# Delta attention: block products two at a time on 64x64 corners, all five instruction queues in a new order, and an opening block with four operand buffers

## The reference, cut to what matters

```
q, k, v = silu(short_conv(x @ Wq)), silu(short_conv(x @ Wk)), silu(short_conv(x @ Wv))
beta = 2 * sigmoid(x @ Wb);  g = -exp(A_log) * softplus(x @ Wa + dt_bias)
q = q * rsqrt(sum(q*q) + 1e-6) / sqrt(128);  k = k * rsqrt(sum(k*k) + 1e-6)
for each token t:
    S = S * exp(g_t)
    for i in range(3):
        S = S + beta_i * outer(k_i, v_i - k_i @ S)
    o_t = q_t @ S
o = o * rsqrt(mean(o*o) + 1e-5) * rms_weight * silu(x @ Wg);  y = o @ Wo
```

## Time and profile before

| | us |
|---|---|
| median of 3 runs | 3219.11 (3215.27 to 3219.3) |
| the profiled execution, its own time | 3221.68 |
| its span | 3219.9 |
| PE busy | 3008.8 (93%) |
| DVE busy | 2537.5 (79%) |
| ACT busy | 2250.6 (70%) |
| POOL busy | 1972.9 (61%) |
| the opening block ends | 78.9 |
| the loop's last output tile | 2478 |

### The profile page before, as it was taken

One profiled execution on the slowest core, in us unless ns is written; L12 is line 12 of the kernel. 1 busy time (PEld: TensorE's weight loads), 2 busy tenths in 40 slices (PEclk: granted clock), 3 DMA queues, 4 the chain that ended last, 5 costly groups with the idle time before them and its releaser, 6 DMA issues. The chain is left out here.

```text
span 3219.9 us, 83441 instructions
## 1 busy us (share of the span) xinstructions
PE 3008.8 (93%) x27212; PEld 2368.3 (74%) x27212; DVE 2537.5 (79%) x5859; ACT 2250.6 (70%) x6953; POOL 1972.9 (61%) x3125
## 2 busy tenths in 40 slices
PE   5569999999999999999999999999987999767999
PEld 3458888888888888888888888888876444455444
DVE  5669999999999999999999999999754454594554
ACT  4768888888888888888888888888643343412443
POOL 1588888888888888888888888888831000100000
PEclk8779999999999999999999999999998899967999
DMA  4457777676777667676767677777532333002322
GB/s 102 122 143 172 180 190 178 172 180 169 179 178 188 179 175 179 174 175 176 187 176 182 173 176 179 175 178 184 151 93 74 148 123 124 10 3 76 145 116 112
DMA packets 588204, 482.87 MB, mean 150 GB/s; under 512 B 464784, under 2 KB 504368, under 8 KB 581632
## 3 DMA queue, kind: packets, MB, share of 16 engines
q1 hardware_dynamic: 583552, 475.44, 55.3%
q10 hardware_dynamic: 4224, 2.10, 0.2%
HBM read 285.53 MB, written 191.86 MB: 148 GB/s over the span
## 5 line engine op out<-in xcount | busy, mean ns | idle before, releaser
L919 DVE SCALAR_TENSOR_TENSOR conv_k<-PP,tk,conv_k 128x256 f32<-128x256 f32 x1536 | 722.6, 479 | 61.0 <-ACT conv_k L754 33.3
L692 POOL TENSOR_TENSOR X<-X,tmp 96x31 f32<-96x31 f32 (+15 forms) x992 | 534.5, 539 | 77.8
L919 DVE SCALAR_TENSOR_TENSOR conv_v<-PP,tv,conv_v 128x256 f32<-128x256 f32 x1152 | 539.3, 477 | 45.0 <-ACT conv_v L754 35.3
L689 POOL TENSOR_TENSOR tmp<-At,X 96x31 f32<-96x31 f32 (+15 forms) x992 | 486.6, 491 | 63.6 <-DMA At<-n_d 5.4
L1088 PE MATMUL PP<-xn,wk 128*128 128x268 f32 x1024 | 342.7, 419 | 35.3 <-DVE conv_k L919 26.5
L675 POOL TENSOR_TENSOR rk<-ss,half 96x8 f32<-96x8 f32 x128 | 209.1, 1633 | 175.4 <-DVE ss L887 175.4
L657 POOL TENSOR_TENSOR Sg<-S,gend 128x512 f32<-128x512 f32 x256 | 266.1, 1040 | 63.3 <-DVE S L878 63.3
L726 ACT ACTIVATE recA<-TG,es 96x128 f32<-96x128 f32 x1024 | 284.8, 368 | 6.0 <-DVE es L912 6.0
L754 ACT ACTIVATE conv_k<-PP,tk 128x256 f32<-128x256 f32 x512 | 245.2, 480 | 56.2 <-PE PP L1088 49.0
L718 ACT ACTIVATE recA<-TG 128x128 f32<-128x128 f32 x1024 | 265.5, 272 | 24.5 <-PE TG L1139 24.5
L1052 PE MATMUL RB<-rhs,Yf 96*96 96x128 f32 x2048 | 269.1, 274 | 14.5 <-DVE rhs L867 14.3
(11 more groups left out here) (289 smaller groups left out, 6776.1 us busy)
## 6 DMA issues: line engine op xcount, KB each, us to landing
kqg_d<-kqgA SPq DMA_DIRECT2D x128, 512.0 KB, 6.2
kqgB<-kqg_d SPq DMA_DIRECT2D x128, 512.0 KB, 4.3
rec_d<-recA SPq DMA_DIRECT2D x128, 480.0 KB, 3.4
recB<-rec_d SPq DMA_DIRECT2D x128, 480.0 KB, 5.6
f1gates<-f1gates_d SPq DMA_DIRECT2D x24, 1024.0 KB, 6.7
f2gates<-f2gates_d SPq DMA_DIRECT2D x24, 1024.0 KB, 6.8
gdec<-gdec_d SPq DMA_DIRECT2D x128, 128.0 KB, 5.6
apk_d<-apkA SPq DMA_DIRECT2D x128, 128.0 KB, 3.3
```

Of the source, the lines that this page charges most:

```text
L689: nc.gpsimd.tensor_tensor(t, At[q % 2][:, j, j + 1:].unsqueeze(2).broadcast_to(sh), X[q % 2][:, j, 0:cols].unsqueeze(1).broadcast_to(sh), ...
L692: nc.gpsimd.tensor_tensor(x, x, t, ALU.subtract).then_inc(sub_ev, 1)
L919: return nc.vector.scalar_tensor_tensor(acc, src[:, :, j:j + SPAN], w[:, j:j + 1], acc, ALU.mult, ALU.add)
```

## The change

In the opening block: `gm` has four buffers instead of two; the fourth piece of each head's table is stored from ACT's queue instead of SP's; the order of squares, copies, turns, centring and norms of the four blocks changes. In the loop: `apkB` and `Dd` hold half of the units on partitions 64 to 127, `zm` does its products in turn on partitions 0 to 63 and 64 to 127 (inputs and outputs), its load is six DMAs instead of three, and `zev` copies in four instructions instead of two. `ss_` adds a tensor of 1e-6 (`g.tiny`) instead of the constant. All five queues have a new order in the frame; `o_(r, 1)`, `mo_(r, 1)`, `vtr(c, 0)`, `vr(c, 0)` and two spots of `subst` pass into the next frame.

```diff
-        gm = sb("gm", [128, 2, NC, TC])
+        DEEP = 4
+        gm = sb("gm", [128, DEEP, NC, TC])
...
+
+        def keep_table(eng, h, b):
+            eng.dma_start(g.edec_d[h, :, :, b, :], ex[TC * b:TC * (b + 1), h, :].rearrange("t (s x) -> t s x", x=SPAN)).then_inc(g.edec_out[h], 16)
...
         @block.sync
         def _(sp):
...
             for h in range(NH):
...
-                for b in range(B):
-                    sp.dma_start(g.edec_d[h, :, :, b, :], ex[TC * b:TC * (b + 1), h, :].rearrange("t (s x) -> t s x", x=SPAN)).then_inc(g.edec_out[h], 16)
+                for b in range(B - 1):
+                    keep_table(sp, h, b)
...
+            raw(2)
...
-            raw(2)
+            raw(3)
...
-            raw(3)
...
+            gates(2)
...
-            gates(2)
...
-                    last = nc.tensor.matmul(GE[h % 2][:, a, :], after_bd[:, :], gm[:, h % 2, 16 * a:16 * (a + 1), :], start=True, stop=True)
+                    last = nc.tensor.matmul(GE[h % 2][:, a, :], after_bd[:, :], gm[:, h % DEEP, 16 * a:16 * (a + 1), :], start=True, stop=True)
...
         @block.scalar
...
             for q in range(B):
+                square(q)
...
-                square(q)
-                if q:
-                    keep_xn(q - 1)
+                if q >= 2:
+                    keep_xn(q - 2)
+            keep_xn(B - 2)
...
             for h in range(NH):
...
+                if h:
+                    act.wait_ge(mask_ev, h)
+                    keep_table(nc.scalar, h - 1, B - 1)
+            act.wait_ge(mask_ev, NH)
+            keep_table(nc.scalar, NH - 1, B - 1)
...
         @block.gpsimd
         def _(pool):
...
+            nc.gpsimd.memset(g.tiny[:, :], 1e-6)
...
             for q in range(B):
...
             for q in range(1, B):
...
+                centre(q)
...
-                centre(q)
-                norm(q - 1)
+                if q >= 2:
+                    norm(q - 2)
+            norm(B - 2)
...
             def sums(h):
...
-                need(dve, ge_mm, h - 2)
-                nc.vector.tensor_tensor(gm[:, h % 2, :, :], gt[:, h, :].unsqueeze(2).broadcast_to([128, NC, TC]), upto, ALU.mult).then_inc(gm_ev, 1)
+                need(dve, ge_mm, h - DEEP)
+                nc.vector.tensor_tensor(gm[:, h % DEEP, :, :], gt[:, h, :].unsqueeze(2).broadcast_to([128, NC, TC]), upto, ALU.mult).then_inc(gm_ev, 1)
...
-            sums(0)
-            sums(1)
+            for h in range(DEEP - 1):
+                sums(h)
             for h in range(NH):
...
-                if h + 2 < NH:
-                    sums(h + 2)
+                if h + DEEP - 1 < NH:
+                    sums(h + DEEP - 1)
...
 
         kqgB = two("kqgB", [128, U, 128])
         recB = two("recB", [R, U * 128 + U * TC])
-        apkB, Dd = two("apkB", [64, U, 64]), two("Dd", [64, U, 64])
+        apkB, Dd = two("apkB", [128, HU, 64]), two("Dd", [128, HU, 64])
         Yf = two("Yf", [R, U, R])
         Zt = sb("Zt", [R, U, 64])
         vt = sb("vt", [128, U, R])
...
                 need(sp, zm_mm, N - 2)
                 sp.wait_ge(preset_ev, 1)
                 sp.wait_ge(st_ap[N % 2], 4 * uses(N))
-                sp.dma_start(apkB[N % 2][:, :, :], apk_d[slot(N)]).then_inc(ld_da[N % 2], 16)
+                for hf in range(2):
+                    sp.dma_start(apkB[N % 2][64 * hf:64 * hf + 64, :, :], half(apk_d[slot(N)], hf)).then_inc(ld_da[N % 2], 16)
                 sp.wait_ge(st_x[q % 2], uses(q))
                 for b in range(2):
                     o = slice(BLK * b, BLK * (b + 1))
-                    sp.dma_start(Dd[N % 2][o, :, o], x_d[q, lanes(N, b)].rearrange("u r c -> r u c")).then_inc(ld_da[N % 2], 16)
+                    for hf in range(2):
+                        rows = slice(64 * hf + BLK * b, 64 * hf + BLK * b + BLK)
+                        sp.dma_start(Dd[N % 2][rows, :, o], x_d[q, lanes(N, b)][hf * HU:(hf + 1) * HU].rearrange("u r c -> r u c")).then_inc(ld_da[N % 2], 16)
 
             def y_load(N):
                 if not live(N):
...
 
             for f in range(NF):
                 r, c = f - BACK - 1, f - BACK
+                rec_load(c)
                 at_load(*group_at(f, GROUP + 1))
                 x_store(*group_at(f, 2 * GROUP + 1))
-                rec_load(c)
+                dec_load(f)
                 da_load(c + 1)
                 weights(*divmod(f, KSTEPS))
-                dec_load(f)
-                kqg_store(f - 1)
+                y_load(c + 1)
                 rec_store(f - 1)
                 ap_store(f - 1)
-                y_load(c + 1)
+                kqg_store(f - 1)
 
         @block.gpsimd
         def _(pool):
...
             nc.gpsimd.memset(S[0][:, :, :], 0.0).then_inc(preset_ev, 1)
             for f in range(NF):
                 r, c = f - BACK - 1, f - BACK
+                fo_(r - 1)
+                sg(r, 0)
+                subst(*group_at(f - 1, GROUP + 1), range(10, 12))
+                kqg(f - 1)
+                rk_(f - 1)
+                sg(r, 1)
+                subst(*group_at(f, GROUP + 1), range(0, 9))
                 x_zero(*group_at(f, 3))
-                fo_(r - 1)
-                kqg(f - 1)
-                sg(r, 0)
-                rk_(f - 1)
-                subst(*group_at(f, GROUP + 1), range(0, 6))
-                sg(r, 1)
-                subst(*group_at(f, GROUP + 1), range(6, 12))
+                subst(*group_at(f, GROUP + 1), range(9, 10))
 
         @block.scalar
         def _(act):
...
                 need(act, zm_mm, N)
                 need(act, m3_mm, N - 1)
                 act.wait_ge(preset_ev, 1)
-                nc.scalar.activation(Zt[32:64, :, 0:32], ZW[0:32, :, 0:32], ACT.Copy, scale=-1.0)
-                nc.scalar.activation(Zt[64:96, :, :], ZW[32:64, :, :], ACT.Copy, scale=-1.0).then_inc(zev_ev, 1)
+                for hf in range(2):
+                    nc.scalar.activation(half(Zt, hf)[32:64, :, 0:32], ZW[64 * hf:64 * hf + 32, 0:HU, 0:32], ACT.Copy, scale=-1.0)
+                    last = nc.scalar.activation(half(Zt, hf)[64:96, :, :], ZW[64 * hf + 32:64 * hf + 64, 0:HU, :], ACT.Copy, scale=-1.0)
+                last.then_inc(zev_ev, 1)
 
             def w12(N):
                 if not live(N):
...
 
             for f in range(NF):
                 r, c = f - BACK - 1, f - BACK
-                xt(*group_at(f, 2 * GROUP + 1))
                 tap0(c, "v0")
+                mo_(r - 1, 1)
+                ksum_(f - 1, 1)
                 tap0(c, "v1")
-                ksum_(f - 1, 1)
                 ksum_(f - 1, 0)
                 wev(r, 0)
                 tap0(c, "v2")
+                xt(*group_at(f, 2 * GROUP + 1))
                 gate_(c)
                 zev(c)
                 tap0(f, "k1")
                 mo_(r, 0)
                 tap0(f, "k0")
+                kr(f - 1, 1)
                 kr(f - 1, 0)
+                w12(c)
+                q2_(f - 1)
+                tap0(f, "k2")
+                tap0(f, "q")
                 vsilu(c)
-                kr(f - 1, 1)
-                tap0(f, "k2")
-                w12(c)
                 wev(r, 1)
-                q2_(f - 1)
-                tap0(f, "q")
-                mo_(r, 1)
                 yev(c)
                 ksilu(f)
                 qsilu(f)
...
                     need(dve, ksum_ev[hf], N)
                 need(dve, rk_ev, N - 1)
                 need(dve, q2_ev, N - 1)
-                nc.vector.tensor_scalar(ss[:, :], ksum[:, :], 1e-6, None, ALU.add).then_inc(ss_ev, 1)
+                nc.vector.tensor_tensor(ss[:, :], ksum[:, :], g.tiny[:, :], ALU.add).then_inc(ss_ev, 1)
 
             def rinv_(N):
                 if not live(N):
...
             for f in range(NF):
                 r, c = f - BACK - 1, f - BACK
                 tap1(c, "v0")
+                tap2(c, "v0")
+                vr(c - 1, 0)
+                tap3(c, "v0")
                 osb_(r - 1)
-                tap2(c, "v0")
                 rhs_(r, 0)
-                tap3(c, "v0")
                 tap1(c, "v1")
                 og_(r - 1)
                 tap2(c, "v1")
...
                 ss_(f - 1)
                 rinv_(f - 1)
                 acc_(r - 1)
+                step_(f - 1)
                 tap1(c, "v2")
-                step_(f - 1)
                 tap2(c, "v2")
                 tap3(c, "v2")
+                es_(f - 1)
                 sup(r, 0)
-                es_(f - 1)
                 tap1(f, "k1")
+                tap2(f, "k1")
                 tap1(f, "k0")
                 tap2(f, "k0")
                 tap3(f, "k0")
+                tap3(f, "k1")
                 rhs_(r, 1)
-                tap2(f, "k1")
-                ap(f - 1, 0)
-                tap3(f, "k1")
+                ap(f - 1, 1)
                 tap1(f, "k2")
                 tap2(f, "k2")
-                ap(f - 1, 1)
                 tap3(f, "k2")
                 tap1(f, "q")
                 tap2(f, "q")
                 tap3(f, "q")
```

(27 more changed lines are left out.)

## The result

Before and after were timed beside each other: 3219.2 us (median of 4 runs, 3215.27 to 3219.44) against **3315.07 us** (4 runs, 3311.54 to 3317.86). The ratio is **1.0294, 95% interval 1.0281 to 1.0307**: slower by 96 us, where 41 us less were forecast. The profiled execution took 3313.82 us, with a span of 3312.0.

The account below looks back on a forecast made before the run. PE's instruction stream was taken as the bound, with one ACT stall each fourth frame. Steady 13 + opening 13 + fill 3 + drain 12 = 41 us off 3219.1 gave 3178; own range 3150 to 3208, whole range 3132 to 3232.

Parts of the forecast that it names:

- That the pair overlaps: `zm` on PE: two row halves run at once, slot 1.08 to 0.54 us, saving 0.54 per frame.
- PE's frame of 17.21: PE's work in a steady loop frame: 17.52 - 0.54 (pair) + 0.23 (tile switching) = 17.21 us.
- the switch: PE, `o_(r,1)` split from `m3`: entering and leaving small tiles adds 0.23 us per frame, bounds 0 and 0.3.
- SP's order, "Cost 0": SP's queue: `kqg_store` behind the other stores delays nothing; n_d lands before POOL's first subst at about 10.6; cost 0.
- `mo`, `fo_`, `osb_` hidden, 0.9 to spare: Steps after `o_(r-1,1)` in the frame: osb done at 3.5 us, `ot` needs it at 4.4, so no wait.
- The tensor addition: `ss` on DVE beside POOL's `kqg` multiplies: held 0.4 us, bounds 0.4 and 1.07; 0.1 us per normal frame.
- the rival's 0.7: Rival, `ss` on DVE waits for both POOL multiplies: 0.7 us per normal frame, 3231 us; chance 0.1.
- xt ahead of the gate: ACT's `xt` before `gate_` each fourth frame: PE's k1 stalls 1.25 us instead of 0.75; long frame 18.4 to 18.6.
- `zev` and the loads, "Cost 0": ACT pays at most 0.6 us more, covered by `wm` 2 us later; three more SP loads at most 2.6; cost 0.
- Opening block 13: Before the loop: 7 us from norm, transposes and gates, about 6 from table stores; 13 taken, bounds 8 and 15.
- Drain 12, fill 3: Loop's ends: 1.15 us saved in each of 11 drain frames, 12 us; fill saves 3 as `xt` lets squares pass.
- The rival with the right place: Rival, `ss` on DVE between tap3 v1 and tap1 v2 waits for both POOL multiplies: 3231 us; chance 0.1.

Follow-up runs that it names:

- both edits: Changed kernel with SP's At load issued ahead of the recurrence's load again and the `ss` addition done by ScalarE (ACT): 3206.14 us, ratio 0.9953.
- the tensor-scalar: Changed kernel with the constant of `ss` added by the tensor-scalar form of before, in the same place on DVE: 3318.86 us, ratio 1.0302.
- the order of before: Changed kernel with all five queues' main loops put back in the kernel before's order; pair, opening block and tensor constant stay: 3196.23 us, ratio 0.9920.
- the pair alone: Kernel before with only the paired block products (`zm`, `zev` and their loads) of the change: 3206.00 us, ratio 0.9953.
- At first: Changed kernel with SP's load of At issued ahead of `rec_load` again: 3245.02 us, ratio 1.0069.
- `ss` on ACT: Changed kernel with the key norms' constant added by ScalarE behind its second sum, no longer by VectorE: 3281.49 us, ratio 1.0184.
- `xt` in halves: Changed kernel with all five queues in the kernel before's order, `xt` copied in two halves and SP's store of the second result moved: 3188.99 us, ratio 0.9900.

## Why the prediction was wrong

**That the pair overlaps: right.** Slot 0.61 against the forecast 0.54, in one PSUM bank with two row tiles on different partitions. The rule of the Trainium skill that the prediction weighed (TensorEngine Tiling (Array Packing), Restrictions and Gotchas) would have given 1.08; the measurement decides against it for this case. The saving is 0.47 and not 0.54 on the slot, and 0.42 on the short frame.

**PE's frame of 17.21: the right terms, a little small.** 17.40 measured. 0.07 from the slot, 0.07 from the switch (0.23 taken, 0.30 measured, the bound). The last 0.05 wasn't traced.

**SP's order, "Cost 0": the step that failed.** I looked at when the stores behind At are issued and wrote that n_d lands before POOL's first step at about 10.6. I did not ask what now stands ahead of the At load: `rec_load`, which the diff moves in front of it in plain sight, with 992 KB. It lands 6.9 us after its issue, and POOL, which starts the group with it, loses 2.89 us, where the prediction had no wait. With the one load put back in its place it lands in 3.9, POOL's wait is gone, and the time is 70 us less. I had gone through the queue for the stores and not for the loads.

**"`mo`, `fo_`, `osb_` hidden, 0.9 to spare": failed as a consequence.** The spare time held against PE and ACT (with both edits PE never waits at `ot`), but POOL's queue in front of `fo_` was taken as empty. When At is late, the frame's last steps of substitution run past the point where `fo_` is due.

**The tensor addition: right mechanism, wrong size.** I took 0.4 us of hold, the bound was 1.07, and the median is 1.08, the most 1.82. The nearest row that I chose, `step_` with 0.48, stood beside a single POOL operation; `ss` stands beside two with no gap, and the row of the fill with 1.66 us showed exactly that. The cost was 34 to 39 us, between the two: my 0.1 us in 88 normal frames is 9, the rival's 0.7 is 62. That the form doesn't matter was in the prediction, and the tensor-scalar confirms it; both forms are held alike, as its sentence on the Trainium skill's page (GPSIMD Engine Reference, the table of SBUF interfaces) had it.

**xt ahead of the gate: right.** Forecast 1.25 us of stall in a frame of 18.4 to 18.6; measured 0.99 in one of 18.66 once the other waits are away.

**`zev` and the loads, "Cost 0": right on PE in the short frames, open in the long one, wrong in the drain.** ACT is busy 440.1 us in 500 with the order of before, against 429.4: 0.33 more per frame by the durations of the copies, and it stands in the same stretch as `xt`. Whether it is this or PE's shorter frame that uncovers ACT wasn't separated. In the drain the cover of 2 us that I counted on is gone: from 2260 to 2470 us PE waits for `Zt` at `wm` 11 times in the kernel with the order of before (3.6 us) and 11 times in the one with both edits (6.5 us, once 1.8), and never in the kernel before. At full clock a drain frame is 15.49 us with the pair in the old order and 15.14 without it.

**Opening block 13: 7.7.** z came at 33.0 and not 31.5. The stores were costed at 0.70 each on SP, 16.8 in all, and took 20.6: I assumed that a store costs its queue the same when another queue stores too. Up to 2.6 us of the 7.7 can be chance, as the run with the pair alone shows.

**Drain 12, fill 3: about 2.5 and a loss of 2.5.** Of `osb`'s transposes, the kernel before and the changed one (first and last start at the end):

```profile
L1195 PE MATMUL SD<-ident,osb x256: 272/288/331, 254.4 to 2477.0; 128*128 128x128 f32 x128
```

```profile
L1216 PE MATMUL SD<-ident,osb x256: 272/327/477, 249.2 to 2567.9; 128*128 128x128 f32 x128
```

From the first k tile to the first `ot` it was 175.5 and is 178.0; it is 178.8 with At first, 177.7 with `ss` on ACT and 175.8 with both edits, so the 3 us forecast for the fill came out in none; from the last k tile, at 2285 and 2378, to the last `ot` 192.0 and 189.5. The last frames are 14.14 us as forecast, the first ones of the drain are not: from 2260 to 2470 us PE waits 9.5 us for `osb` and 2.7 for `Zt`.

**The sum.** Forecast -41. By the runs: the late At +70, the held `ss` +39, and what is left -13 (3206 against 3219), where my sum without its 9 for `ss` would have left -50. What is left is, in the spans of the kernel with both edits, 7.0 in the opening, 9 behind the 110th `ot`, and nothing in the steady frames: 1771 us for 100 of them, as before, as the pair's gain is eaten by the switch and by the long frame. So even without its two misplaced instructions the new order gains nothing there; the pair in the old order does. The rival with the right place, `ss` held by both multiplies, gave 3231 and had a chance of 0.1. That a second queue could be late at the same time, through one misplaced load, was in no case, and the range ended 83 us too low.

## What to carry to other kernels

When a diff reorders a queue of DMAs, write down for each load the bytes that are now issued ahead of it and its first user, not only when its data are ready: 992 KB ahead of one load of 384 KB cost more than the whole change was meant to gain. A tiny VectorE operation is not tiny beside a run of GpSimd operations without a gap: price it to the end of the run. And judge parts and order apart: here the new parts with the old order beat both kernels, by under 1% (0.992, and 0.990 with `xt` in halves).

## What the runs showed that I had not expected

**The clock can lengthen the end of the loop.** In the drain PE has gaps. Eighty microseconds of it, up to about 4 us ahead of the last `ot`, in the kernel before, in the one with both edits, and in the one with the order of before and xt in halves, in three fences:

```profile
2393.00:2473.00 80.00, 69.90 (x727) 59.54 (x726) 41.06 (x82) 30.65 (x70) 15.78 (x21) 0.96 0.24 65
```

```profile
2377.00:2457.00 80.00, 73.45 (x800) 60.47 (x799) 48.29 (x96) 36.12 (x88) 17.68 (x24) 1.00 0.30 80
```

```profile
2360.00:2440.00 80.00, 69.16 (x665) 58.11 (x664) 40.38 (x81) 28.90 (x71) 14.29 (x19) 0.90 0.24 63
```

The granted clock is 0.96, 1.00 and 0.90 of full speed (2.4 GHz), so in the last the lower level of 1.2 GHz held for part of each frame. It is seen in single slots. PE's timeline of the last kernel, and of the one without the split, the same eight transposes of v:

```profile
2376.33 1.94 PE L1188 MATMUL TG<-ident,vt 128*96 128x128 f32 x8
2378.07 1.65 PE L1089 MATMUL RA<-ws,recB 96*128 96x128 f32 x8
```

```profile
2381.87 1.08 PE L1179 MATMUL TG<-ident,vt 128*96 128x128 f32 x8
2382.79 1.06 PE L1080 MATMUL RA<-ws,recB 96*128 96x128 f32 x8
```

Both pairs come right after the frame's two longest waits, 0.78 us for rhs and 0.68 for ws. Drain frames are 17.06 us in the first and 15.49 in the second (17.05 in its last ones), with the same PE instructions; six frames of 1.57 us are 9.4 of the 9.7 us that the split gave back. Why one falls to the lower clock in every frame and the other only in the last few wasn't settled. It isn't the amount of work on PE alone: the kernel with both edits has the same products in another order, and in its stretch above it stays at full clock.

**A held addition misses the gap between two POOL operations, but not always.** Above, `ss` waited for the end of the second multiply. One frame earlier, in the long one, it did not; `ss` on DVE, and the multiply that was on POOL when it started, of the changed kernel:

```profile
1511.98 0.28 DVE L906 TENSOR_TENSOR ss<-ksum,tiny 128x8 f32<-128x8 f32 x1
```

```profile
1510.66 1.58 POOL L658 TENSOR_TENSOR kqgA<-kq,gdec 128x768 f32<-128x768 f32 x1
```

It ends at 1512.26, with the first multiply (1512.24), though the second follows at once. In the next frames (1.81 and 1.09 us) it started 1.1 us and 0.4 us ahead of the first one's end and sat out both. The Trainium skill (SBUF — State Buffer, Who interferes with whom) calls what the two engines share an exclusive lock; that fits an operation of 8 elements that takes 0.16 us alone and up to 1.82 us there. Over the whole changed kernel 88 of the 128 additions end with the second multiply, 29 with the first, and 11, in the fill, meet neither. The 29 are one in each group of four, always in the frame with `xt`, and the same holds with At first and with the tensor-scalar. The start doesn't decide it: the 29 start 0.20 to 0.55 us ahead of the first multiply's end, the 88 start 0.19 to 1.11 us ahead. What does wasn't settled.

**Two queues of small stores don't add up**: 24 stores took 0.86 us each on SP while ACT's queue issued 8, and 32 took 0.70 each by themselves.
